# Cross-attention and mixture of experts on one core: the 64-key half tile moves to the middle of a group, queries are made in stacked blocks, and attention outputs are divided before they are projected

## The reference

```python
x = x + xattn(_layernorm(x), ctx, Wq, Wk, Wv, Wo, bo)
#   q, k, v = x@Wq, ctx@Wk, ctx@Wv, cut into 16 heads; sim = q k^T / 8; out = softmax(sim) v; out @ Wo + bo
x = x + ffn(_layernorm(x), ...)
#   sigmoid router, 2 of 4 groups, then 4 of 32 experts, weights normalised times 2.5;
#   silu(t @ gate) * (t @ up) @ down for every expert, weighted; plus a shared expert
```

## Time and profile before

| what | value |
|---|---|
| median of 3 runs | 3225.38 us |
| profiled execution, its own time | 3223.51 us |
| its span, first to last instruction | 3221.7 us |
| TensorE busy | 99%, mean granted clock 0.997 |
| VectorE, ScalarE, GpSimd busy | 74%, 63%, 41% |
| head, to the first group's scores | 42.05 us |
| 63 groups, from scores of step 2 to the same of the last group | 47.31 to 2881.35 us |
| experts, first matmul | 2920.45 us |

### The profile page before, as it was taken

How to read it: one execution, slowest core, us unless ns; L and a number is a source line. 1 busy time by engine, 2 the same in 40 slices (tenths; PEclk the granted TensorE clock), 3 DMA queues, 4 the chain that set the end, 5 groups by cost and what they waited for, 6 DMA issues and landing times.

```text
span 3221.7 us, 40836 instructions
## 1 busy us (share of the span) xinstructions
PE 3179.9 (99%) x15118; PEld 2534.7 (79%) x15118; DVE 2389.6 (74%) x4882; ACT 2017.8 (63%) x2356; POOL 1333.2 (41%) x894
## 2 busy tenths in 40 slices
PE   7999999999999999999999999999999999999999
PEld 5777777778777777778777777777877778777787
DVE  5777777777777777777777777777777777777766
ACT  4666666666666666666666666666666666676555
POOL 5333443334333343334443344333433334225566
PEclk8999999999999999999999999999999999999999
DMA  2000000000000000000000000000000000105553
GB/s 82 1 17 1 17 1 1 18 1 18 1 18 1 18 1 1 17 1 18 1 18 1 18 1 18 1 1 18 1 18 1 18 1 1 40 3 122 120 129 76
DMA packets 31707, 67.48 MB, mean 21 GB/s; under 512 B 8339, under 2 KB 9620, under 8 KB 31124
## 3 DMA queue, kind: packets, MB, share of 16 engines
q1 hardware_dynamic: 31508, 64.88, 7.8%
HBM read 61.72 MB, written 2.62 MB: 20 GB/s over the span
## 4 chain that ended last, share of the span: by engine, by line
PE 96%; DVE 1%; POOL 1%; issue 1%; ACT 0%; DMA 0%; POOLq 0%; SPq 0%; DVEq 0%; ACTq 0%
PE st L593 12%; PE st L596 12%; PE side L535 11%; PE op L606 11%; PE op L612 11%; PE st L599 11%; PE op L609 11%; PE side L629 3%; PE st L716 2%; PE st L718 2%; PE st L717 2%; PE side L528 1%; PE op L620 1%; PE op L623 1%; PE side L530 1%; PE side L529 1%
## 5 line engine op out<-in xcount | busy, mean ns | idle before, releaser
L473 POOL TENSOR_TENSOR p_lo<-p_full,p_hi 128x1024 fp32r<-128x1024 f32 x320 | 819.7, 2562 | 1753.1 <-ACT p_hi L877 1753.1
L1156 DVE TENSOR_REDUCE m_part<-side 128x1 f32<-128x400 f32 x2016 | 1072.7, 568 | 502.3 <-PE side L535 502.2
L874 ACT ACTIVATE p_full<-st 128x1024 f32<-128x1024 f32 x768 | 788.8, 1027 | 876.8 <-PE st L599 848.5
L877 ACT ACTIVATE p_hi<-st 128x1024 fp32r<-128x1024 f32 x768 | 784.9, 1022 | 0.0
L1139 DVE TENSOR_TENSOR p_lo<-p_full,p_hi 128x1024 fp32r<-128x1024 f32 x448 | 545.5, 1218 | 85.6 <-ACT p_hi L877 85.6
L535 PE MATMUL side<-cT_hi,qT_hi 96*128 96x400 f32 x2016 | 554.5, 346 | 0.0
L593 PE MATMUL st<-qT_hi,cT_hi 97*128 97x512 f32 x1664 | 540.8, 406 | 11.9 <-DMA qT_hi<-m_row 11.1
L596 PE MATMUL st<-qT_lo,cT_hi 96*128 96x512 f32 x1664 | 524.3, 396 | 0.0
L606 PE MATMUL op<-p_hi,v_hi 128*97 128x512 f32 x1536 | 487.6, 398 | 1.6 <-DVE p_lo L1139 1.6
L612 PE MATMUL op<-p_hi,v_lo 128*97 128x512 f32 x1536 | 480.4, 394 | 0.0
L609 PE MATMUL op<-p_lo,v_hi 128*97 128x512 f32 x1536 | 480.4, 394 | 0.0
(11 more groups left out here) (171 smaller groups left out, 3072.1 us busy)
## 6 DMA issues: line engine op xcount, KB each, us to landing
w_rep<-w_rows SPq DMA_DIRECT2D x64, 512.0 KB, 6.6
keys_nat<-in_ctx_keys SPq DMA_DIRECT2D x16, 672.0 KB, 6.0
keys_tur<-in_ctx_turned SPq DMA_DIRECT2D x16, 600.4 KB, 4.8
gud_raw<-in_moe_w SPq DMA_DIRECT2D x2, 1152.0 KB, 7.7
out_x<-x SPq DMA_DIRECT2D x8, 256.0 KB, 2.0
x<-in_x SPq DMA_DIRECT2D x1, 1920.0 KB, 12.7
qT_hi<-m_row SPq DMA_DIRECT2D x64, 4.0 KB
oT<-e_row SPq DMA_DIRECT2D x64, 4.0 KB
```

The costliest lines, as they stand in the source:

```text
L473: pool.tensor_tensor(p_lo[:, slot(s), :], p_full[:, s % 2, :], p_hi[:, slot(s), :].bitcast(F32), ALU.subtract).then_inc(s_lo_pool, 1)
L874: act.activation(p_full[0:m, s % 2, :], made, ACT.Exp, scale=SCALE)
L877: act.activation(p_hi[0:m, slot(s), :], made, ACT.Exp, scale=SCALE).then_inc(s_ex, 1)
L1156: dve.tensor_reduce(m_part[:, k % NT, k // NT:k // NT + 1], where[:, 0:MAXW], AX.X, ALU.max).then_inc(s_drain, 1)
```

## The change

1. **Half tile mid-group.** It becomes step 6 (`HALF = 6`, `tile_of`, `step_of`); the score banks alternate by `(n + s) % 2`, since 13 is odd. `POOL_STEPS` becomes 3, 5, 7, 9, 12.
2. **Stacked queries.** The four heads' 96 rows are put in three blocks of 128 rows (the fourth head in thirds under the other three): 9 matmuls where there were 12. ScalarE and VectorE take them apart again, in 3 and 2 pieces where there was 1 and 1.
3. **Outputs divided and projected at once.** The denominators of a group are gathered by two DMAs as 64 x 16, added and inverted on VectorE, stored to DRAM and spread back over 96 partitions (`send_denominators`, `spread_inverted`). VectorE multiplies (`divide_first`, `divide_last`), ScalarE and VectorE split hi and lo, and one job Z of 9 fp32r matmuls of 256 columns projects all four heads. Z adds into `y_sum`; once a batch V turns it back and it is added to the tokens. The Y jobs go.
4. **Low halves read last.** `weigh` does the two products with `p_hi` before it waits for `p_lo`.
5. **Small steps behind the projection's sum.** Layer-norm and routing steps on VectorE run behind Z, or after the next group's first `lo`.
6. **Shorter head.** GpSimd no longer waits for the second weights before it shifts the context; the maxima row's DMA is issued before the next context is loaded; the last weights are multiplied after the maxima.
7. The last batch's jobs move from chunk 0 to chunk 1, its routing to chunk 2.

```diff
-        PLACES = {2: ("MM", "M"), 3: ("MM", "M"), 4: ("MM", "MM"), 5: ("MM", "M"), 6: ("MM", "MM"),
-                  7: ("MM", "MM"), 8: ("MM", "MY"), 9: ("MM", "MM"), 10: ("MM", "MM"), 11: ("YY", "YT"),
-                  12: ("QQ", "")}
+        PLACES = {2: ("MM", "MM"), 3: ("MM", "M"), 4: ("MM", "MM"), 5: ("MM", "M"), 6: ("M", "MM"),
+                  7: ("MM", "MM"), 8: ("MM", "MM"), 9: ("MM", "MM"), 10: ("MM", "M"), 11: ("", "T"),
+                  12: ("", "", "ZQQ")}
...
+            def send_denominators(g):
                 sp.wait_ge(s_el, g + 1)
+                sp.dma_start(den[:, 1, :], e_row[:, g % 2, :].rearrange("a (c d) -> a c d", d=16)).then_inc(s_dl, 16)
+                sp.wait_ge(s_oe, g + 1)
+                sp.dma_start(den[:, 0, :], oT[DC:OW, :].rearrange("o (a b) -> o a b", b=16)).then_inc(s_dl, 16)
+            def spread_inverted(g):
+                sp.wait_ge(s_rc, 2 * g + 2)
+                sp.dma_start(r_rows[g % 2].rearrange("(a b) -> a b", b=16), inverse[:, :]).then_inc(s_rd, 16)
+                sp.wait_ge(s_rd, 16 * (g + 1))
+                sp.wait_ge(s_on, g)
+                sp.dma_start(r_rep[:, :], r_rows[g % 2:g % 2 + 1, :].to_broadcast([DC, GQ])).then_inc(s_rr, 16)
+            send_max_row(J0_T + 1, 0)
             load_context(1, NGB)
-            send_max_row(J0_T + 1, 0)
...
             def project_queries(where, g, half, k):
-                for h in range(2):
-                    head = g * GH + 2 * k + h
-                    o = where[0:DC, h * NQ:(h + 1) * NQ]
+                for block in ((0, 1), (2,))[k]:
+                    o = where[:, block % 2 * NQ:(block % 2 + 1) * NQ]
...
+            def project_outputs(where, g):
+                pe.wait_ge(s_ol, g + 1)
+                for k in range(3):
+                    pe.matmul(where[:, 0:NQ], B_hi[:, i, k, :], o_hi[:, k, :], start=(k == 0), stop=False)
+                    pe.matmul(where[:, 0:NQ], B_lo[:, i, k, :], o_hi[:, k, :], start=False, stop=False)
+                    mm = pe.matmul(where[:, 0:NQ], B_hi[:, i, k, :], o_lo[:, k, :], start=False, stop=(k == 2))
...
                 pv(S - 2)
+                side_jobs(at[S - 1][2])
...
+                for into, made in unstacked(qT_hi[slot], where, k):
+                    ins = act.activation(into, made, ACT.Copy)
...
+            def divide_first(g):
+                dve.wait_ge(s_rr, 16 * (g + 1))
+                dve.tensor_tensor(o_all[0:DC, :, :].rearrange("p k t -> p (k t)"), oT[0:DC, 0:3 * NQ],
+                                  r_rep[:, 0:3 * NQ], ALU.mult)
+            def divide_last(g):
+                for k in range(3):
+                    third = slice(k * DT, (k + 1) * DT)
+                    ins = dve.tensor_tensor(o_all[DC:P, k, :], oT[third, 3 * NQ:GQ], r_rep[third, 3 * NQ:GQ], ALU.mult)
```

More of the change, by code:

```diff
@@ L587, in _, with scores @@
             turn_maxima(bank(J0_T))
-            def scores(s, slot, par):
-                keys = slice(s * P, s * P + P)
+            multiply_weights(6, op)
+            multiply_weights(7, op)
+            def scores(n, s, slot, par):
+                tile = tile_of(s)
+                keys = slice(tile * P, tile * P + P)
+                halves = [slice(j * BANK, (j + 1) * BANK) for j in range(2)]
+                into = st[:, (n + s) % 2]
+                for j in range(2):
+                    pe.matmul(into[:, j, :], cT_hi[par][:, keys], qT_hi[slot][:, halves[j]], start=True, stop=False)
+                for j in range(2):
+                    mm = pe.matmul(into[:, j, :], cT_hi[par][0:DC, keys], qT_lo[slot][:, halves[j]],
+                                   start=False, stop=(s == HALF))
+                for j in range(0 if s == HALF else 2):
+                    mm = pe.matmul(into[:, j, :], cT_lo[par][:, keys], qT_hi[slot][0:DC, halves[j]],
+                                   start=False, stop=True)
+                mm.then_inc(s_qk, 1)
@@ L591, in scores, with weigh @@
+            def weigh(g, s, par):
+                tile = tile_of(s)
                 halves = [slice(j * BANK, (j + 1) * BANK) for j in range(2)]
                 for j in range(2):
[L593 to L597 removed]
@@ L598, in scores @@
-                for j in range(2 if s < FULL else 0):
-                    mm = pe.matmul(st[:, s % 2, j, :], cT_lo[par][:, keys], qT_hi[slot][0:DC, halves[j]],
-                                   start=False, stop=True)
-                mm.then_inc(s_qk, 1)
-            def weigh(s, par):
-                halves = [slice(j * BANK, (j + 1) * BANK) for j in range(2)]
-                for j in range(2):
-                    pe.matmul(op[0:OW, j, :], v_hi[par][:, s, :], p_hi[:, slot(s), halves[j]],
+                    pe.matmul(op[0:OW, j, :], v_hi[par][:, tile, :], p_hi[:, slot(s), halves[j]],
@@ new lines, in divided_lo, with add_outputs @@
+            def divided_lo(g):
+                dve.wait_ge(s_oh, g + 1)
+                dve.tensor_tensor(o_lo[:, :, :], o_all[:, :, :], o_hi[:, :, :].bitcast(F32),
+                                  ALU.subtract).then_inc(s_ol, 1)
+            def add_outputs(where, filled, g):
+                dve.wait_ge(s_fill, filled)
+                if g % NGB:
+                    dve.tensor_tensor(y_sum[:, :], where[:, 0:NQ], y_sum[:, :], ALU.add).then_inc(s_drain, 1)
+                else:
+                    dve.tensor_copy(y_sum[:, :], where[:, 0:NQ]).then_inc(s_drain, 1)
```

543 lines of the change are left out of this document (325 added, 218 removed).

## The result

The changed kernel takes **3180.74 us** (median of four runs, 3180.20 to 3181.69) against 3225.99 (3225.15 to 3226.61) for the kernel before: a ratio of 0.9861 (95%: 0.9850 to 0.9873), 45 us or 1.4% faster. The forecast was 3166 with a range of 3143 to 3208.

What follows compares the result with a forecast made beforehand. TensorE, busy 99%, was taken as the bound. From 3223.5 us, 68 - 16 + 6 - 2 + 2 + 1 = 59 us less gave 3164.5 profiled, 3166 as a median; range 3143 to 3208.

Steps and rivals of the forecast that it cites:

- TensorE's work, -1.08 a group: TensorE per group: Y jobs, fp32 returns and three query matmuls go, Z and V come; 1.08 us less, 68 over 63 groups.
- gaps of 0.25: New TensorE waits per group, between 0 and 1.0 us, taken as 0.25: 16 us lost over 63 groups.
- seam's side banks: Where groups meet, TensorE fills the side banks while VectorE is busy 6.9 us, then waits 0.1 to 0.4 us.
- free wide loads: Stationary operands of 128 columns, where queries had 96, were taken to cost 0; 28 us was kept as an end.
- ScalarE at the seam: Where groups meet, ScalarE needs some 4.3 us before TensorE wants the score bank at 4.5: 0.2 us left.
- rival 2: ScalarE bounds the place where groups meet, each group waiting 1.0 us, not 0.25: 47 us lost, 3213; chance 0.13.
- rival 3: VectorE bounds the place where groups meet, side banks stopping TensorE; at 1.5 a group 79 us lost, 3245; chance 0.06.
- the rule on quadrants: VectorE instruction starting in another 32-partition quadrant waits until all before it finish; the assumed 0.41 us a piece already holds it.
- Head: Start of kernel: earlier GpSimd shift and maxima row start step 2 near 41 us; 6 us gained, between 1 and 9.
- Once: End of group 0: the sum over B grows from one reduction to five instructions; 2 us lost.
- Last group: It ended in a half tile with a 2.9 us wait; a full tile leaves 0.5: 2 us gained.
- Experts: Four fp32 jobs leave chunk 0, Z and V enter chunk 1: 1 us gained, within 3.

Runs made afterwards that it cites:

- experiment 7: The changed kernel with the nine matmuls of the projection job Z issued twice: 3251.71 us, ratio 1.0084 to the kernel before.
- experiment 8: The changed kernel with Z's stationary operands cut from 128 to 96 columns, leaving out 32 model dimensions: 3182.10 us, ratio 0.9869 to the kernel before.
- experiment 1: The changed kernel with the sum over B's five instructions spread over steps 4 to 10 of group 0: 3177.49 us, ratio 0.9851 to the kernel before.
- experiment 2: The changed kernel with GpSimd's B_lo in group 1 behind step 5's piece, not step 9's: 3178.83 us, ratio 0.9853 to the kernel before.
- experiment 12: The changed kernel with its weighing order and its place for VectorE's small steps both undone: 3322.94 us, ratio 1.0302 to the kernel before.

## Why the prediction was right, and where it was off

- **TensorE's work, -1.08 a group, and gaps of 0.25.** Together -0.83; measured -0.81. The new gaps came to some 0.35, nearly all at maxima (38.7 us of the loads' waits), so the work fell by 1.16. Two misses of about 0.1 cancel, and that is luck. The places of the gaps are right in one part only. By the spacings 0.19 lies at step 8, two steps behind the half tile, as I had it (0.1 to 0.2); but of the 0.1 to 0.4 that I had put at the seam's side banks none stands at the first maxima of a group, and some 0.18 lies at steps 4, 6 and 7, for which I had no term. Z's 1.07 is confirmed by experiment 7 (1.08), the free wide loads by experiment 8.
- **ScalarE at the seam had 0.2 left.** It kept TensorE waiting for nothing there; rival 2 did not come. In the group shown above, its second exponential of step 0 ends at 1424.48 and TensorE starts on that bank at 1424.74: 0.26 left. **VectorE at the seam** (rival 3) neither: the small steps and the queries' low parts end before TensorE asks. The pieces are not cheap: in that group the five of the queries' low parts take 2.46 us from the first start to the last end, for 2.39 as the sum of their lengths, where the two of 96 x 512 of the kernel before overlapped (1.27 for 1.35). That is in line with the rule on quadrants that the prediction names. But how little room there was I had not seen. The change is not a saving of 68 less 16; it is a saving that exists only with three orders around it. Undoing the weighing order costs 50, the small steps' place 44, the two 142, the half tile's place 0.86 a group (54) in the better of two arrangements. I priced the first at "0.93 more for `lo`" without asking what it holds up, and the half tile only as 0.1 to 0.2 lost.
- **Head, 6 gained: 4.8, and half of the mechanism wrong.** GpSimd's early start and the row of maxima came as I had said, the row later (issued at 35.95 and not near 34). What I had wrong is what holds step 2: I had ScalarE's copies and two exponentials in front of it, and half of the 5.3 us at the lower clock as gained. But ScalarE waited for TensorE, whose scores of steps 0 and 1 ran without a wait from 37.96 to 43.22, 5.26 us at a clock of 0.50, just as long as before (42.05 to 47.31). The lower clock gave nothing back; up to step 2 the gain is the row's alone, 42.05 - 37.96 = 4.1, and 0.7 more fell within group 0.
- **Once: the step that failed.** "The sum over B at the end of group 0 grows from one reduction to five instructions ...: I take 2 lost." Spreading it gave 5.6 (experiment 1): the five take 6.3 us, for 3.92 before, and behind the wait of 4.28 come seven us at the slow clock, which I had reckoned in the head and not here. And B_lo on GpSimd (4.6, experiment 2) is in no term. By the table, the two stretches behind T of group 0 lost 7.9 + 0.8 and the gain of two groups, 1.6: 10.3 us, where I had 2. That is 8.3 of the 17 us between my 59 and the 41.8 between the two spans, half of the miss; the last group and the experts make 3 each, the head 1.2. (The median stands 15 above the 3166 of the forecast.)
- **Last group, 2 gained: 1.0 lost.** I expected the half tile's wait of 2.9 to go. One of 1.5 for its low part (L694) stayed, and one of 1.1 for `p_lo` came; no experiment was spent on it, and the cause of this loss stays open. **Experts, 1 gained: 2.0 lost**, within the scatter below.

## What to carry to other kernels

When the bottleneck engine is busy to 99%, a saving on it is only as large as the slack of the engines that feed it: write down, for each operand that it waits for, how much later it could come, and test by delaying one. Weigh once-only work that a new layout needs by what it is queued in front of, and by what runs beside it on the other engine, not by its length. With two buffers between producer and consumer, a third job in a row waits for what is left of the consumer's latency, and for whatever the consumer has in front of it, so moving even one job is to be checked against what stands around it on both engines.

## What the runs showed of the hardware

- One two-input VectorE instruction from SBUF beside one two-input GpSimd instruction from SBUF took 4.25 us for 0.94 (experiment 2 undoes it). In the changed kernel's trace GpSimd's low half takes 2.62 us in the 128 cases where a low half of VectorE began before it and ran on beside it for 0.36, and 2.40 in the other 192.
- A load of 128 columns lasts 190 ns and of 96 columns 161, and with 256 moving columns both give a start every 0.118 us (experiment 8).
- VectorE takes 423 to 427 ns for 32 x 256 and 424 for 128 x 256 (`y_sum`): these pieces cost by their columns, not their partitions. ScalarE the same: 379 for 32 x 256, 384 for 128 x 256.
- TensorE's granted clock was 1.00 behind a wait of 1.60 us and fell to 0.50 (1.2 GHz) behind one of 4.28; in experiment 12 it fell at the weigh of step 11 in 7 of 60 groups.
- The stretch from the first expert matmul to the last took 299.2 to 303.4 us in the ten traces of kernels whose code there is the same (but for the narrower last Z of experiment 8), the changed kernel's among them. A difference of 2 us between two single traces says nothing there.
